# First router of a fused transformer kernel: logits computed with the tokens on the partitions

## The reference, cut to what matters

```python
# x: 8 x 512 tokens of 128 channels, after a layer norm; E = 8 experts, K = 2, CAP = 512, H = 512
logits = jax.nn.relu(x @ rw1 + rb1) @ rw2 + rb2        # (4096 tokens, 8)
vals, ids = jax.lax.top_k(logits, K)
probs = jax.nn.softmax(vals, axis=-1)
m = jax.nn.one_hot(ids_f, E, dtype=jnp.int32)
pos = jnp.cumsum(m, axis=0) - 1                        # place of each pick in its expert's list
keep = (pos_tok < CAP).astype(x.dtype)
disp = jnp.zeros((E, CAP, Cx), x.dtype).at[ids_f, pos_c].add(xr * keep[:, None])
```

## Time and profile before

| | |
|---|---|
| time, median of 3 runs | 906.22 us (905.99 to 906.40) |
| profiled execution | 906.78 us |
| its span | 905.0 us |
| mean granted TensorE clock | 0.966 of full speed |
| busy share of the span, PE, PEld, DVE, ACT, POOL | 85%, 52%, 76%, 70%, 70% |
| PE busy, 227.2 to 237.5 us of the span (one batch of the stage) | 10.3 us of 10.3 |

### The profile page before, as it was taken

How to read it: one execution, slowest core, us unless ns; L and a number is a source line. 1 busy time by engine, 2 the same in 40 slices (tenths; PEclk the granted TensorE clock), 3 DMA queues, 4 the chain that set the end, 5 groups by cost and what they waited for, 6 DMA issues and landing times. The chain is left out here.

```text
span 905.0 us, 18379 instructions
## 1 busy us (share of the span) xinstructions
PE 772.4 (85%) x6152; PEld 468.8 (52%) x6152; DVE 684.2 (76%) x2029; ACT 629.4 (70%) x972; POOL 630.8 (70%) x416
## 2 busy tenths in 40 slices
PE   3978656678998799288889989999999999999997
PEld 1344212224443366132235757777777777777775
DVE  7859999975775587598999878666767666666654
ACT  3755333414445587168889988898989888889895
POOL 5008999810677546466998997686868686868695
PEclk9979898999999799689999999999999999999999
DMA  5899400018100120442600000000000000000000
GB/s 152 118 119 185 147 0 0 18 27 236 33 16 7 44 63 25 126 112 56 196 1 1 1 3 1 13 0 12 0 12 0 12 0 12 0 0 12 0 14 13
DMA packets 52794, 40.48 MB, mean 45 GB/s; under 512 B 6060, under 2 KB 44735, under 8 KB 52735
## 3 DMA queue, kind: packets, MB, share of 16 engines
q1 hardware_dynamic: 49662, 37.28, 18.7%
q0 software_dynamic: 3072, 2.51, 1.0%
HBM read 18.07 MB, written 14.88 MB: 36 GB/s over the span
## 5 line engine op out<-in xcount | busy, mean ns | idle before, releaser
L759 POOL TENSOR_TENSOR scratch<-scratch 128x1024 f16<-128x1024 f32 x128 | 272.8, 2134 | 84.6 <-ACT scratch L1216 82.4
L1877 DVE SCALAR_TENSOR_TENSOR resid<-PS,coef,resid 128x128 f32<-128x128 f32 x512 | 144.0, 344 | 108.7 <-PE PS L1929 103.2
L1929 PEld LDWEIGHTS PS<-A,scratch 128*128 128x128 f16 x3456 | 203.4, 98 | 37.8 <-POOL scratch L759 4.8
L1929 PE MATMUL PS<-A,scratch 128*128 128x128 f16 x3456 | 217.1, 219 | 3.9 <-POOL scratch L759 1.6
L1929 PE MATMUL PS<-A 128*128 (+1 forms) x768 | 186.8, 379 | 0.7 <-issue 0.2
L1212 ACT ACTIVATE scratch<-PS,cols 128x512 f32<-128x512 f32 x256 | 163.8, 683 | 25.8 <-PE PS L1929 18.9
L1216 ACT ACTIVATE scratch<-scratch 128x1024 f16<-128x1024 f32 x128 | 135.3, 1057 | 5.0
L1929 PE MATMUL PS<-scratch,ident 128*128 128x512 f32 x160 | 85.0, 651 | 41.1 <-DVE scratch L1392 41.0
L624 POOL TENSOR_TENSOR scratch<-A 128x1024 f32<-128x1024 f32 x32 | 75.7, 2393 | 59.1 <-DVE A L1363 56.7
L1929 PEld LDWEIGHTS PS<-A 128*128 128x128 f16 x768 | 70.7, 98 | 66.5 <-issue 0.7
L669 POOL DMA_INDIRECT disp<-A,scratch x64 | 62.9, 982 | 36.5 <-issue 30.1
(11 more groups left out here) (342 smaller groups left out, 1332.9 us busy)
## 6 DMA issues: line engine op xcount, KB each, us to landing
A<-A SPq DMA_DIRECT2D x22, 256.0 KB, 7.5
y_rows<-zeros SPq DMA_DIRECT2D x8, 512.0 KB, 6.0
A<-y_rows SPq DMA_DIRECT2D x14, 256.0 KB, 3.9
disp<-zeros SPq DMA_DIRECT2D x4, 528.0 KB, 21.3
resid<-in_L_attn_x SPq DMA_DIRECT2D x8, 256.0 KB, 3.8
A<-scratch SPq DMA_DIRECT2D x8, 256.0 KB, 7.2
A<-in_L_ffn_ew SPq DMA_DIRECT2D x1, 2048.0 KB, 12.7
A<-scratch SPq DMA_DIRECT2D x32, 64.0 KB, 2.0
```

The source lines that it names most:

```text
L759: pool.tensor_tensor(h_low[n % 4], h_full[n % 2], h_high[n % 4], SUB).then_inc(S("m1_low"), 1)
L1877: last = STT(out=resid[:, g, :], in0=bank(4 + e % 2)[:, t * C:(t + 1) * C], scalar=coef[b % 2][:, t, e:e + 1], in1=resid[:, g, :], op0=MUL ...
L1929: return nc.tensor.matmul(o, l, r, start=start, stop=stop)
```

## The change

The logits are computed at once with the tokens on the partitions: for each of the 4 token tiles, 4 matmuls (one for each slice h of the hidden layer) have the 128 x 128 tile of the hidden layer stationary and the router's 8 columns moving, and write 128 x 8 into bank 5. The transposed logits, ScalarE's copy of them, the 4 small transpositions and the semaphores `lgT5_mm` and `lg5_T` go. `router_logits(b)` stands where `router_logits_T(b)` stood, ahead of `transpose5(b + 1)`. `relu5` and `route` wait for `lg5_mm`, `route` reads bank 5, the new matmuls wait for `lg5_added` of the batch before, and ScalarE gets a wait for its own last rectified slice before it writes weights into PSUM at the end of the stage.

```diff
             def relu5(b, h):
                 n = b * HC0 + h
-                act.wait_ge(S("lgT5_mm"), at(b, 2))
+                act.wait_ge(S("lg5_mm"), at(b, 2))
                 act.wait_ge(S("hid5_mm"), at(n))
...
-            def lgT5_copy(b):
-                act.wait_ge(S("lgT5_mm"), at(b))
-                act.wait_ge(S("lg5_mm"), at(b, 1))
-                A_(lg5_T, bank(5)[0:E0, :], ACT.Copy).then_inc(S("lg5_T"), 1)
...
-                lgT5_copy(b)
                 if b + 1 < B:
                     xT5_copy(b + 1)
...
+            act.wait_ge(S("hid5"), at(B * HC0 - 1))
             for k in range(EARLY):
                 weights0_beside(k)
...
                 dve.wait_ge(S("lg5_mm"), at(b))
-                TT(lg5[u], bank(6)[:, 0:NT * E0].rearrange("p (n e) -> p n e", e=E0),
+                TT(lg5[u], bank(5)[:, 0:NT * E0].rearrange("p (n e) -> p n e", e=E0),
...
-            def router_logits_T(b):
+            def router_logits(b):
                 pe.wait_ge(S("hid5"), at(b * HC0 + HC0 - 1))
-                pe.wait_ge(S("lg5_T"), at(b, 1))
-                for h in range(HC0):
-                    last_mm = mm(bank(5)[0:E0, :], w_r2[:, h, :], hid[b % 2][:, h, :], start=h == 0, stop=h == HC0 - 1)
-                last_mm.then_inc(S("lgT5_mm"), 1)
-
-            def router_logits(b):
-                pe.wait_ge(S("lg5_T"), at(b))
-                pe.wait_ge(S("placed"), at(b, 1))
-                for t in range(NT):
-                    last_mm = nc.tensor.transpose(bank(6)[:, t * E0:(t + 1) * E0], tile(lg5_T, t), ident[0:E0, 0:E0])
+                pe.wait_ge(S("lg5_added"), at(b, 1))
+                for t in range(NT):
+                    for h in range(HC0):
+                        last_mm = mm(bank(5)[:, t * E0:(t + 1) * E0], tile(hid[b % 2][:, h, :], t), w_r2[:, h, :],
+                                     start=h == 0, stop=h == HC0 - 1)
                 last_mm.then_inc(S("lg5_mm"), 1)
...
-                router_logits_T(b)
+                router_logits(b)
                 if b + 1 < B:
                     transpose5(b + 1)
                 if b and b + 2 < B:
                     variance_o(b + 2)
-                router_logits(b)
```

More of the change, by code:

```diff
@@ L128, in build @@
                     "r0_decay", "r_coef", "p2_copied", "o_sq", "o_std", "x_std",  "hid5",
-                    "rows5", "lg5_T", "m0_hid",  "m1_cT", "m1_hid", "m1_high",
+                    "rows5", "m0_hid",  "m1_cT", "m1_hid", "m1_high",
                     "xn7",  "kq_high", "v_copied7", "gk_copied", "sg_7", "gate_ln", "gate_high",
@@ L136, in build @@
                     "gate_low", "yg1_ready", "z_added",   "mlp_added", "xn12", "split_low", "m0_low", "xdT", "x_low", "lg12_added", "lg_less", "z_stats", "hid11_low"],
-            "pe": ["transposed", "proj_q", "proj_k", "proj_b", "proj_g", "proj_v", "ss_head", "r0_acc", "r_q", "r_acc", "p2_mm", "centred", "o_var", "proj_o",  "hid5_mm", "lgT5_mm", "lg5_mm", "counts", "trd",
+            "pe": ["transposed", "proj_q", "proj_k", "proj_b", "proj_g", "proj_v", "ss_head", "r0_acc", "r_q", "r_acc", "p2_mm", "centred", "o_var", "proj_o",  "hid5_mm", "lg5_mm", "counts", "trd",
                    "m0_hid_mm", "m0_out_mm", "m1_cT_mm", "m1_hid_mm", "m1_out_mm", "m1_bias_mm",  "kq_mm", "v_mm7", "g_mm7", "gk_mm", "r1_k", "r1_e",
@@ L380, in build @@
         id5 = [v.rearrange("p (k n) -> p k n", k=TOP0) for v in routing(192, 8)]
-        lg5_T = carve(8)[0:E0, 512:1024]
         place = by_expert(carve(8)[:, 0:32])
```

## The result

The changed kernel takes 922.08 us in the median of 4 runs (918.63 to 922.79), the kernel before 906.31 us beside it: a ratio of 1.0157, 95% interval [1.0143, 1.017]. It is slower by 15.8 us, where 12.5 were forecast. The profiled execution took 922.79 us, its span is 921.1 us.

A forecast was written before the change was run, and what follows sets the result against it. It took GpSimd, VectorE and TensorE, in one 10.5 us rhythm, as the bound. Seven clock falls at 2.5 less 0.5 us make 14.0, less 1.5 gained: 906.22 + 12.5 = 918.7 us, range 908 to 928.

The forecast's parts named there:

- What bounds the stage: Stage at 197 to 312 us: GpSimd, VectorE and TensorE go in one rhythm of 10.5 us a batch.
- The passes: New logits on TensorE: 32 passes at 0.111 us, 3.56 us at full clock, about the same as the 3.60 removed.
- The shift at full clock: From 221.98 us on, everything moves 0.95 us earlier, because `route` of batch 0 starts earlier.
- That the clock falls, once in a batch: TensorE's 4.9 us of logits, transpositions and variance move few columns, so its clock drops in each batch; chance 0.78.
- The price of a fall: TensorE, each batch: 5 us at half speed loses 2.5 us, of which slack covers 0.5; seven make 14.0 us.
- Batch 0: `route` there starts 0.95 us earlier; its thin stretch is one of seven, each losing 2.5 us less 0.5 of slack.
- a fall that catches the start of the next logits: Low clock reaching into the following batch's logits on TensorE: 3 us, counted only in the upper bound of +17.
- What GpSimd gains at full clock: Scatters: about 1.5 us earlier, no more, since the first scatter of a batch needs the slots.
- What the profile was to show: Signs: 0.50 clock each batch, 12 to 13 us rhythm, fifth scatter waiting for logits, first expert's rows transposed at 327 us.
- Loads that hold the clock, the first: Rival: dense weight loads count as work, TensorE keeps its clock, 904.7 us (903.6 to 908.9); chance 0.16.
- The second, few falls: Rival: the clock drops in a few batches only, 3 x 2 - 1.5 = +4.5, 910.7 us; chance 0.04.
- the third, a clock that never returns: Rival: the clock drops and stays low until the stage is over, +47, 953 us; chance 0.02.

## Why the prediction was right, and where its size was off

**What bounds the stage.** Right: the three engines go in one rhythm, and a delay of TensorE's showed in full at the stage's end.

**The passes.** Right: 3.74 us for 32 at full clock, 0.117 us each, against 0.111 taken. Cold they take 0.22 us, as the 1-column passes of the earlier trace rows had it. The shift at full clock is borne out by 64 columns with plain writes: from the same start of the stage (197.56 and 197.58 us) the logits of batch 1 begin 0.80 us earlier and those of batch 2 0.93, where I had 0.95. (`lg5_added` is some 4.6 us old when TensorE asks, 243.43 against 248.06 in the kernel before, and not 7; it costs nothing either way.)

**That the clock falls, once in a batch.** Right, and shown: 8 low stretches between 215 and 325 us, and, with plain writes, a clock of 1.00 from 221 to 293 us with 64 columns moving against 0.79 with 8. The inference that weight loads do not hold the clock, which I had called the open point, is borne out by the kernel with 64 columns. The rule that I had weighed against it (Trainium skill, TensorE: Matmul & The Clock Gate, the table on why this matters), which ties the drop to pauses between bursts, does not agree with the trace here: TensorE was busy for 71.93 of 72 us at a granted 0.75, and for 67.48 of 72 at 1.00 before.

**The price of a fall.** I took 2.5 us less 0.5 of slack, 2.0 for each. The logits of batch 1 began 2.9 us later than before, those of batch 7 16.0 us later (305.85 instead of 289.88): 13.1 us over six batches, 2.2 for each. The term was right to a tenth, with luck in it. The six low stretches between those two starts lasted 6.3 us on average and not 5, a loss of 3.1 at half speed; of that 0.95 was absorbed and not 0.5, as TensorE had stood idle for 4.5 of 72 us, 0.66 in a batch, besides the 0.33 of the small transpositions. The seven low stretches that began ahead of batch 7's logits lasted 3.4 to 10.2 us, where I had bounded them by 3.4 (a value that no row of the kernel before shows for a low stretch) and 5.5, and the starts of the logits lie 11.5 to 14.4 us apart instead of an even 12 to 13.

**Batch 0** is the term that was mis-sized. I had 0.95 us gained there by the earlier `route`, then one fall of 2.0 net: 1.05 us later at batch 1. Measured were 2.9. The clock fell at 215.5 us, inside the first logits and not behind them:

```profile
214.09 5.75 PE L1923 MATMUL PS<-w_r,scratch 128*128 128x8 f32 x32 [0.84 <-ACT scratch L897]
219.69 1.09 PE L1930 MATMUL PS<-ident,A 128*128 128x128 f32 x4
...
230.12 4.60 PE L1923 MATMUL PS<-w_r,scratch 128*128 128x8 f32 x32
```

5.75 us instead of 3.6 ahead of `route`, so the gain turned into a loss. The clock was back from 225.7 us on, and the logits of batch 1 began at 1.00; it fell again inside them, at 232.6 us, which makes their 4.60 us. I had named a fall that catches the start of the next logits only as a bound (+3). Since the stage began 0.65 us earlier in this profile than in the one before, counted from its start batch 0 lost 3.5 us and the whole stage 16.8, of which the totals show 16.2; why it began earlier I do not know.

**What GpSimd gains at full clock, and an eighth fall.** I counted 1.5 us, 0.55 more than TensorE's shift, and argued that its first scatter waits for the slots. That is the wait seen, and the gain was there: in batch 6 the slots come 15.3 us later than before (304.55 and 289.21), the first scatter 14.7 (305.49 and 290.81). What I put at nothing is the fall in the logits of batch 7. They are, before and then after:

```profile
289.88 3.60 PE L1929 MATMUL PS<-scratch,w_r 128*8 128x512 f32 x8 [0.84 <-ACT scratch L898]
```
```profile
305.85 5.38 PE L1923 MATMUL PS<-w_r,scratch 128*128 128x8 f32 x32 [0.84 <-ACT scratch L897]
```

The clock falls at 307.7 us, inside them, and the fifth scatter of batch 6 waits 1.73 us for them (312.01) instead of the usual 0.30. This takes the gain back and more: from there on GpSimd is 16.1 us late. Of the 3.6 us by which the last scatter exceeds my 12.5, batch 0 has 1.8, the six batches at 2.18 have 1.1, and the remaining 0.7 come of this eighth fall, where I had counted seven.

**What the profile was to show.** The first expert's rows were transposed at 331.22 us (327 forecast, 315.00 before). GpSimd's fifth scatter was to wait for the logits, and its wait for the slots was listed as a sign of my being wrong. That was a slip in reading my own mechanism: the fall lies between the logits and the counts, so it delays the slots, and the logits, which come ahead of it, are in time. Only in batch 0 and at the end (312.01) does a scatter wait for logits.

**The rivals.** Loads that hold the clock, the first, is refuted on the chip. The second, few falls, and the third, a clock that never returns, did not occur. The kernel with the logits in the old place looks like the third, with 6.97 us for its logits and 0.65 in the stretch, but is not the same: its clock comes back in every batch, and its 53 us over the kernel before (41 over its neighbours) come with engines that no longer overlap. That this is near to the +47 of the third is chance.

## What to carry to other kernels

A TensorE that is never idle can still lose its clock: before turning a matmul round so that its long side becomes the stationary one, look at what the new passes move and at what stands beside them, and read the granted clock of the stretch, not the busy share. Where a pass is as long as its weight load, moving the same columns eight times over cost 0.05 us in 3.74 here and, with signals on time, kept the clock; two and four times did not. The thin passes placed last instead of first in their stretch cost 41 us more. And measure such a change on more than one chip: what cost 1.6% on one was 0.4% on another, where signals between engines came late in the same stage.

## What the hardware showed beyond that

The chips were of two kinds: the kernel before took 906 to 907 us on the first and the last, and 933 to 934 us on the two in between. On the slower kind, signals between engines came some 2 us late in the stage with the scatters (2.1 for the counts above, where the first chip had 0.04), and replacing the 64 scatters of that stage by 32 plain writes took off 21 us (934.34 to 913.37) and left it with a rhythm of 10.4 us. No profile was taken of the kernel before with its scatters on such a chip. That the scatters' own traffic delays the signals is the likely reading, not a shown one: half of the writes went with them, and the same edit of the kernel before was not run on a chip of the faster kind. Whether the changed kernel with 64 columns and its real scatters beats the kernel before on such a chip was not measured either; by the runs with plain writes (-0.5 us in 913) my estimate is within 0.2% of it.
